# Products of the identity in the TensorE gaps of the first graphs of a four-layer graph network

## The reference

```python
h = jnp.maximum(_layernorm(x, axis=-1), 0.0)
x = x + _L0_gnn_ref(h, adj, ...)     # attention, 4 heads: softmax over leaky_relu(e_dst + e_src) where adj > 0.5
h = jnp.maximum(_layernorm(x, axis=-1), 0.0)
x = x + _L1_gnn_ref(h, adj, adj, ...)  # max over 7 relations of A_r @ (h @ W_r)
h = jnp.maximum(_layernorm(x, axis=-1), 0.0)
x = x + _L2_gnn_ref(h, adj, ...)     # degree-normalised convolution, relu
h = jnp.maximum(_layernorm(x, axis=-1), 0.0)
x = x + _L3_gnn_ref(h, adj, ...)     # layer norm, Laplacian product, softplus
```

## Time and profile before

| | us |
|---|---|
| median of 3 runs | 698.53 (697.9 to 700.7) |
| the profiled execution | 699.71 |
| its span, first to last instruction | 697.7 |
| PE busy | 648.7 (93%) |
| ACT busy | 544.8 (78%) |
| DVE busy | 531.5 (76%) |
| POOL busy | 369.2 (53%) |
| mean granted TensorE clock | 0.97 |

### The profile page before, as it was taken

One profiled execution on the slowest core, in us unless ns is written; L12 is line 12 of the kernel. 1 busy time (PEld: TensorE's weight loads), 2 busy tenths in 40 slices (PEclk: granted clock), 3 DMA queues, 4 the chain that ended last, 5 costly groups with the idle time before them and its releaser, 6 DMA issues. The chain is left out here.

```text
span 697.7 us, 20320 instructions
## 1 busy us (share of the span) xinstructions
PE 648.7 (93%) x7476; PEld 525.4 (75%) x7476; DVE 531.5 (76%) x1641; ACT 544.8 (78%) x1271; POOL 369.2 (53%) x435
## 2 busy tenths in 40 slices
PE   5669899999999999999999999999999899998855
PEld 4466778879697878788797878788796768787544
DVE  5776768887878788887878788887878778884641
ACT  5777668888888898888888897988888776865442
POOL 2545565564746565654846465655742564454420
PEclk9589999999999999999999999999999999999996
DMA  7222040222222111222222211222212210200000
GB/s 212 92 59 80 3 137 3 77 77 78 77 78 77 61 39 57 76 78 78 77 77 78 76 50 44 64 79 77 77 62 77 63 53 25 78 2 16 1 15 16
DMA packets 39532, 44.47 MB, mean 64 GB/s; under 512 B 4545, under 2 KB 23050, under 8 KB 39434
## 3 DMA queue, kind: packets, MB, share of 16 engines
q1 hardware_dynamic: 38802, 42.95, 19.7%
q10 hardware_dynamic: 632, 0.22, 0.1%
HBM read 38.83 MB, written 4.33 MB: 62 GB/s over the span
## 5 line engine op out<-in xcount | busy, mean ns | idle before, releaser
L475 POOL TENSOR_TENSOR rstd<-ve,half_neg 128x4 f32<-128x4 f32 (+1 forms) x67 | 89.1, 1329 | 208.1 <-DVE ve L1388 63.9
L797 ACT ACTIVATE side<-d_all,sd 128x512 bf16<-128x512 f32 x256 | 163.8, 713 | 35.3 <-DVE pos L1307 29.3
L1833 PEld LDWEIGHTS ps<-part,pos 128*128 128x128 bf16 x3072 | 101.3, 97 | 9.4 <-issue 6.1
L1833 PE MATMUL ps<-part,pos 128*128 128x66 bf16 x3072 | 103.4, 193 | 0.2 <-DVE pos L1307 0.2
L1307 DVE TENSOR_TENSOR pos<-side,none 128x2048 bf16<-128x2048 bf16 x64 | 80.7, 1260 | 6.1 <-ACT side L797 5.1
L1369 DVE TENSOR_REDUCE best<-ps 128x128 f32<-128x896 f32 x64 | 68.5, 1086 | 12.8 <-PE ps L1929 11.4
L2031 PE MATMUL ps<-u,adj_tr 128*128 128x128 f32 x512 | 62.5, 282 | 3.0 <-ACT u L897 3.0
L2031 PEld LDWEIGHTS ps<-u,adj_tr 128*128 128x128 f32 x512 | 60.6, 198 | 4.3 <-ACT u L897 4.3
L1819 PEld LDWEIGHTS ps<-part,nmask 128*128 128x128 bf16 x1536 | 53.4, 99 | 13.1 <-issue 12.9
L1877 PE MATMUL ps<-adj_tr,h 128*128 128x512 f32 x128 | 58.5, 600 | 0.2 <-ACT h L706 0.2
L1891 PE MATMUL ps<-adj_in,h 128*128 128x512 f32 x128 | 57.8, 593 | 0.0
(11 more groups left out here) (162 smaller groups left out, 1488.0 us busy)
## 6 DMA issues: line engine op xcount, KB each, us to landing
adj_in<-in_adj SPq DMA_DIRECT2D x16, 1024.0 KB, 5.8
d_all<-d_dram SPq DMA_DIRECT2D x64, 256.0 KB, 3.7
x_in<-in_x SPq DMA_DIRECT2D x16, 256.0 KB, 3.0
out_y<-y_out SPq DMA_DIRECT2D x15, 256.0 KB, 2.5
d_dram<-sd_t SPq DMA_DIRECT2D x64, 2.0 KB, 1.4
w_sb<-in_L_gnn_W SPq DMA_DIRECT2D x7, 64.0 KB, 2.2
b_sb<-in_L_gnn_b SPq DMA_DIRECT2D x1, 256.0 KB, 3.2
out_y<-y_out SPq DMA_DIRECT2D x2, 128.0 KB, 1.8
```

Source lines behind the costliest of these rows:

```text
L475: G.tensor_tensor(rstd[:, cut], ve[:, cut], half_neg[:, cut], ALU.pow).then_inc(power, 1)
L797: last = A.activation(side[:, t, :], d_all[:, h, :], ACT.Sign, bias=sd[:, 0, h, t:t + 1])
L1833: last = mm(ps[:, B_HEADS[q] + i // 2, o:o + VAL], pos[h % 2][:, t, i * P:(i + 1) * P], parts[n][:, t, h, :], start=False, stop=(i % 2 == ...
```

## The change

A helper, `idle_products(count, b)`, multiplies the 128x128 float32 identity by itself `count` times into the first 128 columns of bank `b`. Nobody reads the result. It is called at eight places of PE's list, with 154 products in all: 144 by the time graph 2 is projected, and 10 more before the first `h2_transposed`. Three of the calls are preceded by a new wait, which protects the bank written.

```diff
+            def idle_products(count, b):
+
+                for _ in range(count):
+                    mm(bank(b)[:, 0:P], ident[:], ident[:], start=True, stop=True)
...
             mean_value(at(0))
+            idle_products(10, B_SETUP[0])
             top_rows(at(0))
+            idle_products(3, B_SETUP[0])
             top_all(at(0))
             set_up()
             h0_transposed(at(1))
+            pe.wait_ge(adj_sb, at(0).all(T))
+            idle_products(72, B_ADJ[2])
             project(at(1))
             row_sums(at(0))
+            idle_products(8, B_ADJ[2])
             no_edges(0)(at(0))
...
             adjacency(3)(at(1))
+            pe.wait_ge(s_setup, 3)
+            idle_products(36, B_SETUP[0])
             top_rows(at(1))
+            idle_products(10, B_SETUP[0])
             top_all(at(1))
+            idle_products(5, B_SETUP[0])
             project(at(2))
...
             adjacency(3)(at(2))
+            pe.wait_ge(best_ok, at(0).th(3, T))
+            idle_products(10, B_REL[2] + 1)
             h2_transposed(at(0))
```

## The result

The changed kernel takes 710.08 us (median of 4 runs, 709.4 to 711.23), before 698.47; the ratio is 1.0158, 95% interval 1.0137 to 1.0179. It is slower, 11.6 us by the medians. The two profiled executions are 10.56 us apart (710.27 and 699.71).

The account below looks back on a forecast made before the run. PE was taken to set the pace once the pipeline is filled, so its delay by 90 us moves the end. +9.75 - 1.2 = +8.5 us on the median 698.53 gave 707.0 us, range 703 to 714.

Parts of the forecast that it names:

- The price of one product: Each 128x128 float32 product is two records: 0.222 us at full clock, 0.41 us at 1.2 GHz.
- the rival of one record: A product costs one record, 0.111 us, so products fit and the clock gains 2.8 us: 695.7 us; chance 0.08.
- Steps 1 and 2: Set-up: 10 and 3 products put `top_all` 1.0 us late; no clock fall at 18.2; train starts about 20.85 us.
- Step 3: 72 products before graph 1's projection take 16.0 us, to 36.85 us, making that projection 7.65 us late.
- sign of being wrong: A clock row of 0.50 under the train of 72 would make the forecast wrong.
- Steps 4 to 6: First pair gives back 1.48 us; 36 products take 8.0 us; after 10 and 5, PE is 9.65 us late at `product_ah`.
- Step 7: Chain from `s_rel` to graph 1's `no_edges`: starts 11.65 us late, shortens by 1.9, leaving 9.75 us late at 64.74.
- Step 8: 10 products before `h2_transposed` keep the clock up, gaining 1.2 us, with 0 and 1.7 us as ends.
- The rival of the low clock: Products leave the clock low, each taking 0.41 us: about +46 us, 745 us; chance 0.03.

Follow-up runs that it names:

- fitted: The change with product counts that fit their waits at 0.222 us each (5, 1, 29, 0, 15, 6, 3, 6): 701.31 us, ratio 1.0027.
- half kernels: The change with half of each product count (5, 1, 36, 4, 18, 5, 2, 5): 700.22 us, ratio 1.0019.
- the one with transposes: The change with all 154 calls as transposes of the identity instead of float32 products: 700.73 us, ratio 1.0025.
- the bf16 kernel: The change with all 154 products from the identity's bf16 copy, plus a wait for that copy before the first call: 700.75 us, ratio 1.0026.

## Why the prediction was right, and where not

The side, the time (707.0 for 710.08, inside 703 to 714) and the mechanism held: a product is two records, the train overruns its wait, and PE's list carries the delay to the end. That the time came as near as 3.1 us is in part luck: the run carries +12.3 us, not +8.5, and some 2 us of the difference come back at the end of the program, where no step of mine was. Point by point:

- **The price of one product** held: 72 products in 8.04 us (54.02 to 62.06), 0.223 us each. The rate that the Trainium skill gives ("TensorE: Matmul & The Clock Gate", "Back-to-back issue gap"), about 81 ns, does not hold for it, neither per product nor per record (0.111 us); nor does the rival of one record.
- **Steps 1 and 2** held within 0.8 us: `top_all` at 18.32 for 18.2, and no fall at 18.2. The set-up took 0.6 us longer than 20 records of 0.111, so the train began at 21.61 for 20.85. A small misreading was in it: the stretch from 14.4 us shows 1.00, but the transposes up to 14.7 us still ran 0.21 us apart, the pace of the low level. From 14.96 us on the pace is 0.111, so nothing hangs on it.
- **Step 3** was 1.7 us short: the train took 17.7 us and not 16.0, since the clock was at 0.50 for its first 3.4 us. I had taken the high clock as held once PE was busy; here PE was busy and it fell. This is the one sign of being wrong that I had named and that came; what makes the clock fall there stays open.
- **Steps 4 to 6** held in their differences: 1.49 us back in the first pair (1.48), 8.04 us for the 36 (8.0), 2.44 from `top_rows` over the ten to `top_all` (2.3), 1.60 from the projection to `product_ah` (1.6). The whole is later by the 2.5 us of steps 2 and 3.
- **Step 7** was too dear by 0.7 us: the chain from `s_rel` to `no_edges` took 76.17 - 64.91 = 11.26 us for 13.87, shorter by 2.6 and not 1.9.
- **Step 8** failed: -1.2 us forecast, +0.9 measured (+11.4 at 83 us, +12.3 at 105), outside the ends that I gave it. The clock and the gain of 1.2 us at `conv_product` (+10.24) came as forecast; that PE's position there reaches the end did not. I read DVE's `d_low` as the next bound and did not look at the load of features behind it, which DVE waited for at 94.98 us in the profile before as well. The 1.2 us went into a wait of PE (1.59 us at `aht`), which the fixed 9.56 us behind the load show. The 0.9 us are the load itself, 6.08 us for 5.17; what makes it slower is open.
- **The sum.** Of the 12.3 us that the run carries, 8.5 were forecast, 2.5 are from steps 2 and 3, -0.7 from step 7 and 2.1 from step 8, together 12.4. Some 2 us of it came back in the profiled execution at the end.
- **The rival of the low clock** has a slip in its sum: eight products at 0.41 us are 3.3 us, not 2.6. It moves the 745 by 0.7 us.
- **The rival of one record** was mis-sized too. It gave 695.7, a gain of 2.8 us, for products that fit. Four kernels of that kind came out at 1.0019 to 1.0027, with all intervals at or above 1.0000. The clock gain of graph 2's projection is in the rows of all but one of them, and does not reach the end: the next transfer, held by SP's list, takes it up.

Open is why those four are 0.2% slower and not equal. In the fitted and half kernels the clock falls under `product_ah`, behind waits of 3.11 and 3.85 us; in the one with transposes it does not fall, behind a wait of 3.54, and that kernel costs the same. Two times ahead of the scores differ, though. The first `d_all` landed at 22.6 us before and in the bf16 kernel, and at 24.0 to 24.5 in the other three. And the loads of `c_rows` began 13.7 us behind it before and 14.5 to 14.7 in the four, so that they began 0.8 to 2.8 us later, and the scores of graph 1 with them. What sets either time no run here shows.

## What to carry to other kernels

Filler work must be sized by what the same instruction takes in the trace, counted in records and from start to start: the 72 products were twice as long as their wait and put the projection 10 us late, and with half of each count the loss went from 1.6% to 0.2%. Before filling waits to keep a clock up, ask what ends them: where a DMA or another engine's list decides, faster work on the waiting engine only moves the wait. And parts of a change measured alone can add up to less than the whole (here 1.1% for 1.6%), so one of them that looks cheap is not cheap beside the other.

## What the runs showed of the hardware

- The clock fell to 0.50 at 21.6 us in the change, though PE had been busy without a pause since 9.2 us. The last stretch before it, from 18.2 us, held seven narrow float32 products (16 rows by one column). It fell at 23.3 us too, with wide products between the narrow ones.
- A float32 product of 128x128 between products of 16 rows by one column took 0.42 us for 0.222 in a row of its kind, and the narrow one 0.30 for 0.23, at the high clock.
- In a train of float32 transposes the clock came back to 1.00, 5.0 us after the train began, and stayed there.
